# A graph network's edge passes: GpSimd also waits for TensorE's products between the two gathers of a pair

## The reference

```python
deg = jnp.zeros((n,), input_feature.dtype).at[row].add(1.0) + 1.0
dinv = deg ** (-0.5)
norm = (dinv[row] * dinv[col])[:, None]
for l in range(L):                      # L = 5
    xl = h @ W[l] + b[l]
    ee = edge_attr @ We[l] + be[l]      # edge_attr: 53125 x 128
    msg = norm * jax.nn.relu(xl[row] + ee)
    agg = jnp.zeros_like(xl).at[col].add(msg)
    conv = agg + jax.nn.relu(xl + root[l]) / deg[:, None]
    ...                                 # batch norm over the nodes, relu, residual
```

## Time and profile before

| | us |
|---|---|
| median of 3 runs | 5607.82 |
| the profiled execution's own time | 5605.48 |
| its span, first to last instruction | 5603.7 |
| PE busy | 4159.1 (74%) |
| DVE busy | 2968.8 (53%) |
| POOL busy | 2962.8 (53%) |
| ACT busy | 2264.5 (40%) |

### The profile page before, as it was taken

One profiled execution on the slowest core, in us unless ns is written; L12 is line 12 of the kernel. 1 busy time (PEld: TensorE's weight loads), 2 busy tenths in 40 slices (PEclk: granted clock), 3 DMA queues, 4 the chain that ended last, 5 costly groups with the idle time before them and its releaser, 6 DMA issues. The chain is left out here.

```text
span 5603.7 us, 96035 instructions
## 1 busy us (share of the span) xinstructions
PE 4159.1 (74%) x21956; PEld 3397.2 (61%) x21957; DVE 2968.8 (53%) x7177; ACT 2264.5 (40%) x4904; POOL 2962.8 (53%) x3202
## 2 busy tenths in 40 slices
PE   6888828779996777767777677776777767777588
PEld 4555517668885665656666566665656656666455
DVE  5555576652224555555555555555555555555634
ACT  2111136512223444444444444444444444444311
POOL 3666629623333666646666466664666646666142
PEclk8999959879998999989999899898999989999689
DMA  6666638536664444434444344443444434444332
GB/s 206 211 211 210 213 97 222 152 117 182 184 182 127 126 126 129 127 108 127 126 129 127 107 125 126 126 128 105 129 127 126 126 107 130 125 126 127 102 123 80
DMA packets 429338, 782.78 MB, mean 140 GB/s; under 512 B 212572, under 2 KB 269520, under 8 KB 412007
## 3 DMA queue, kind: packets, MB, share of 16 engines
q0 software_dynamic: 136704, 360.53, 23.3%
q1 hardware_dynamic: 281489, 402.18, 22.7%
q10 hardware_dynamic: 11094, 19.50, 1.2%
HBM read 669.16 MB, written 114.48 MB: 140 GB/s over the span
## 5 line engine op out<-in xcount | busy, mean ns | idle before, releaser
L2168 POOL DMA_INDIRECT g_g<-xl_table,g_idx x2080 | 1977.3, 951 | 1322.8 <-issue 556.4
L2202 PE MATMUL g_b<-g_we,g_ea 128*128 128x256 f32 x4160 | 1235.4, 424 | 600.5 <-DVE g_msg L2294 388.5
L2215 PE MATMUL g_b<-g_onehot,g_msg 128*128 128x128 f32 x8320 | 1258.5, 299 | 290.0 <-DVE agg L2307 119.3
L2215 PEld LDWEIGHTS g_b<-g_onehot,g_msg 128*128 128x128 f32 x8320 | 1167.4, 210 | 498.4 <-DVE agg L2307 323.3
L2294 DVE TENSOR_TENSOR g_msg<-g_g,g_b 128x512 f32<-128x512 f32 x1040 | 712.6, 685 | 1061.5 <-DMA g_g<-xl_table,g_idx 590.8
L2202 PEld LDWEIGHTS g_b<-g_we,g_ea 128*128 128x128 f32 x4160 | 776.8, 208 | 767.8 <-DVE g_msg L2294 444.5
L2307 DVE TENSOR_TENSOR agg<-agg,g_b 128x256 f32 x2080 | 864.4, 416 | 418.4 <-issue 167.7
L2258 ACT ACTIVATE g_away<-iota_row,dst_rel 128x128 f32<-128x128 f32 x1040 | 416.5, 400 | 1294.5 <-DMA g_g<-xl_table,g_idx 1127.9
L2276 ACT ACTIVATE g_msg<-g_msg 128x512 f32<-128x512 f32 x1040 | 645.9, 621 | 283.6 <-DVE g_msg L2294 213.6
L544 PE MATMUL sc_pe_h<-ae_h_rows,sc_onehot 128*128 x1664 | 467.3, 428 | 107.2 <-DVE sc_prod L649 103.1
L512 POOL DMA_INDIRECT sc_g<-h_table,sc_idx x416 | 404.6, 973 | 235.5 <-issue 104.6
(11 more groups left out here) (316 smaller groups left out, 3483.1 us busy)
## 6 DMA issues: line engine op xcount, KB each, us to landing
g_ea<-in_ea SPq DMA_DIRECT2D x260, 512.0 KB
ex_w<-in_f_w SPq DMA_DIRECT2D x80, 1024.0 KB
e_rows<-sc_g SPq DMA_DIRECT2D x52, 1088.0 KB
at_g<-e_rows SPq DMA_DIRECT2D x104, 544.0 KB, 4.5
g_g<-xl_table,g_idx POOLq DMA_INDIRECT x2080
xl_table<-g_rows SPq DMA_DIRECT2D x25, 640.0 KB, 3.8
sc_rel<-rel_row ACTq DMA_DIRECT2D x52, 256.0 KB
sc_g<-h_table,sc_idx POOLq DMA_INDIRECT x416
```

Source lines behind the costliest of these rows:

```text
L2168: nc.gpsimd.indirect_dma_start(out=g.g[:, j, :], out_offset=None, in_=k.xl_table[:, :], in_offset=bass.IndirectOffsetOnAxis(ap=g.idx[:, q, ...
L2202: last = nc.tensor.matmul(ep[u % EB][:, i * D:(i + 1) * D], g.ea[:, q, (at + i) * P:(at + i + 1) * P], g.we[:], start=True, stop=True)
L2215: last = nc.tensor.matmul(ps[u % (SB // 2)][:, at:at + P], g.msg[:, j, b * P:(b + 1) * P], g.onehot[:, j, :], start=True, stop=True)
```

## The change

Between the first and the second gather of each pair (`j` odd), POOL waits until PE has counted up `product` for all pairs before the present one, and counts `begun` up. For pair 0 of a pass, where no pair is before, the value is 1, which is the product of pair 0 itself. Inside the loop the value is computed from the loop's register: `it * (BODY // 2) + u`. Nothing else differs.

```diff
-        def gather(u):
+        def gather(u, multiplied):
             for j in (2 * u, 2 * u + 1):
                 q = j // HALF
+                if j % 2 == 1:
+                    pool.wait_ge(g.product, multiplied)
+                    pool.sem_inc(g.begun, 1)
                 nc.gpsimd.indirect_dma_start(
...
-            gather(u)
+            gather(u, max(u, 1))
         with pool.Fori(1, ITERS) as it:
             for u in range(BODY // 2):
...
                 pool.wait_ge(g.summed, it * BODY + 2 * (u - WINDOW + 1) + BODY)
                 pool.sem_inc(g.begun, 1)
-                gather(u)
+                gather(u, it * (BODY // 2) + u)
```

## The result

The changed kernel took 5621.83 us (median of 13 runs, 5613.98 to 5624.72), the one before 5607.64 us beside it (13 runs). The ratio is 1.0025, 95% interval 1.0016 to 1.0033: slower by 14 us, where 52 us were forecast. The profiled execution took 5616.87 us with a span of 5615.1, 11.4 more than the span before.

What follows compares the result with a forecast made beforehand. POOL's gather stream and its pauses were taken to bound the five passes (3265 us). Instructions and prompt waits at zero, late waits +52 us: 5605.5 + 52 + 2.3 = 5660 us, range 5565 to 5745.

Steps and rivals of the forecast that it cites:

- Step 1: Added wait, count and value instructions on POOL between a pair's gathers: hidden, zero taken, 50 us if no cover were left.
- Step 2: Added wait early in a round, where PE's count is prompt: product over 2.7 us ahead, cost nothing.
- Step 3: Added wait late in a round: eights become sevens of 11.10 us, a quarter of sixes become fives of 8.16; +52 us.
- the low bound: Late-count sum over the twelve rounds with no six caught: 74 gathers in 116.8 us, 1.578 each, +35 us.
- The expected signs: Changed profile: pauses before second gathers, 335 becoming 362 at about 2.06 us, sevens for eights, passes some 10 us more each.
- A: No change: the added wait is hidden everywhere on POOL; 5608 us, 0.20 together with the case of a nearly implied wait.
- D: Added wait nearly implied by the first gather's wait for sums, so no change; 0.20 together with the hidden-wait case.
- B: Slower by more: pause falls before the eighth gather but ends no earlier; +133 us, 5741 us, chance 0.13.
- C: Faster: rounds settle at seven, sixes gain a gather at 10.66 us a round; -79 us, 5529 us, chance 0.25.

Runs made afterwards that it cites:

- third set: Unchanged kernel, count of `begun` alone, wait for products two pairs back, and changed kernel, rerun where PE's counts are late; unchanged kernel 5604.84 us.
- the older product: Changed kernel with its added wait asking for products one pair earlier (pair n-2), already implied by the first gather's wait: 1.0060, 1.0003 and 1.0028 on three chips.
- second and fifth: Sets of kernels run on chips with prompt PE counts; the kernel before the change took 4922.02 and 4925.2 us there.
- first, third and fourth set: Sets of kernels run on chips with late PE counts; the kernel before the change took 5654.16, 5604.84 and 5663.92 us there.

## Why the prediction was right in where the pauses go and wrong in what they cost

The sign was right (slower), and so was where the pauses go: they come with PE's late counts, and the added wait moved 112 of 305 of them ahead of second gathers, with L2205 as releaser. Eights gave way to sevens: 127 eights before, 17 after. But the 52 us were to come from this, and the measured 14 us are there without it, in kernels that move no pause. That the sign came out is luck: the term that carries it was put at zero.

**Step 1 failed.** "Zero taken, 50 us if no cover were left" rested on the 0.30 us gaps, which did stay, so nothing could be seen in front of a gather. In the changed kernel the value takes 32 ns and the wait with the count 17 ns, 1000 x 32 + 1040 x 17 ns = 50 us, and none of it lies bare. Yet where the counts are late the instructions are not free: the wait that holds nothing costs 0.28%, the count alone 0.13%, four counts 1.08%. With four counts POOL stops more often, in short gaps and in shorter rounds, and that route was in none of my terms; at the size of the count alone no change of the rounds could be seen. Where the counts are prompt they cost nothing that could be told (1.0003, 1.0001), as step 1 had it. Step 1's zero is right only for that kind of chip.

**Step 2** held. The early gathers of a round restart 0.30 us behind each other as before, and on the chip with prompt counts all but 137 of the 2080 start within 0.4 us (133 gaps up to 1.5 us and 4 longer).

**Step 3 failed in its sum.** The eighth gather was held, as forecast. But a round of seven was to cost 11.10 us and measured 10.79, mainly because the pause grows with the round: from the last start to the restart it is 3.10 us after six and 3.43 after eight in the kernel before, and 3.20 after seven in the changed one (means). I had carried an eight's pause over to a seven, 0.23 us too much. At 1.542 us a gather a seven is as cheap as an eight (1.543), so the term from which all of the +35 us of the low bound came is zero. Fives measured 7.93 us, not 8.16. With these two put into the sum of step 3 and nothing else changed, it is 4 x 10.79 + 5.25 x 9.41 + 1.75 x 7.93 + 6.50 = 112.9 us for 72.25 gathers, 1.5632 us a gather against the 1.5615 of the twelve rounds, and that is some 3 us in place of 52. The third set shows the same by itself: with the older product 1.0028, with the effective wait 1.0031, a difference inside either interval.

**The expected signs.** More pauses came, 335 to about 362 was the forecast; by the count of gaps it was 295 to 305, and by 0.4 us as the limit 346 to 413, of which many are short. The mean fell rather than stay. The passes took 1 to 4 us more each, not 10, and the stages outside them nothing.

**The rivals.** A and D (no change, within 0.2%) fail narrowly where the change was measured, but on the one with prompt counts D is nearly right (1.0011, and the older wait nothing). B, a dearer pause, is refuted by the 10.79 us. C's sevens came, but not shown from sixes: there are 110 eights fewer and 111 sevens more, 52 sixes fewer and 38 fives more, and the rounds can't be followed one by one. A seven cost 10.79 us, not C's 10.66, and the time rose.

What stays open: what physically holds PE's counts while POOL streams gathers, why it happens on some chips and not on others, and why small instructions in POOL's stream bring more pauses there, more in one set than in another (the same kernel with the older product 0.60% and 0.28%). That they lengthen each stream's stretch in which counts are held would fit, but it was only argued. Also untried are the changed kernel without its count, the wait alone ahead of the gather, and the four counts ahead of the pair where counts are late. No kernel here was faster than the one before.

## What to carry to other kernels

An instruction of 17 ns that seems hidden in its engine's queue can still cost time, as here on the chips with late counts; price it by adding four of it, without what it is for, and on a chip of each kind. When a releaser in the profile stands some us after its matmul's row has ended, read when the semaphore counted, and in which stages it is prompt, before a theory is built on buffers. And where a kernel waits in rounds, a wait that splits a pair changes how long the rounds are, so the cost is to be taken per gather from measured rounds of each length, not by moving one pause.

## What the runs showed of the hardware

- PE's semaphore counts came 13 to 15 ns behind the matmul's end in stages without gathers on POOL. In the passes of the kernel before a tenth of `product`'s came 2.8 us or more behind the last row's end, and the traces of the first, third and fourth set show late counts too. On those of the second and fifth they were 14 to 15 ns throughout. The same kernel took 5604.8 to 5663.9 us on the former and 4922.0 to 4925.2 us on the latter. The granted clock was much the same, 0.897 and 0.908.
- The earlier stage that gathers shows it too. PE's counts there come 0.70 us behind the last row's end in the median on the slow kind and 14 ns on the prompt kind. The page's row of its gathers, first on the slow kind (the kernel before), then on the prompt kind.

```profile
L512 POOL DMA_INDIRECT sc_g<-h_table,sc_idx x416 | 404.6, 973 | 235.5 <-issue 104.6
```

```profile
L512 POOL DMA_INDIRECT sc_g<-h_table,sc_idx x416 | 405.2, 974 | 133.3 <-issue 114.2
```

- A gather of 128 rows took 946 ns on POOL with rows of 1032 bytes and 944 with rows of 516, and the next one started 0.30 us behind it. Its last landing count came 1.83 us behind the end of its row on POOL.
- 4000 more instructions of 17 ns on POOL cost 0.01% (interval -0.08 to 0.10) on the prompt kind of chip, and 4160 cost 1.08% on the other; they stood ahead of the pair in the first case and inside it in the second.
